# Capacity experts: routing and slot scatter moved into the preceding attention, results scattered from the slots to the output

## The reference

```python
x = _layernorm(x + _L1_attn_ref(x, ...))      # 16 heads of 8, Gaussian position bias
x = _layernorm(x + _L1_ffn_ref(x, gate_w, w1, w2))

# _L1_ffn_ref: 4096 tokens, 8 experts, capacity 160 slots each
probs = softmax(tokens @ gate_w)
expert_idx = argmax(probs)                     # one expert per token
mask1 = one_hot(expert_idx, E)
pos = cumsum(mask1, axis=0) - 1                # place of the token in its expert's queue
sec_mask = mask1[:, :, None] * one_hot(pos, CAP)    # places from 160 on are dropped
expert_input = einsum('tec,td->ecd', sec_mask, tokens)
h = relu(expert_input @ w1);  expert_output = h @ w2
out = einsum('tec,ecd->td', probs[:, :, None] * sec_mask, expert_output)
```

## Time and profile before

| | |
|---|---|
| median of 3 runs | 1858.01 us (1857.74 to 1858.42) |
| the profiled execution's own time | 1856.96 us |
| its span | 1855.2 us |
| mean granted TensorE clock | 0.936 of full |
| PE busy | 1522.6 us (82%) |
| DVE busy | 1325.1 us (71%) |
| ACT busy | 1047.6 us (56%) |
| POOL busy | 812.4 us (44%) |

### The profile page before, as it was taken

One profiled execution on the slowest core, in us unless ns is written; L12 is line 12 of the kernel. 1 busy time (PEld: TensorE's weight loads), 2 busy tenths in 40 slices (PEclk: granted clock), 3 DMA queues, 4 the chain that ended last, 5 costly groups with the idle time before them and its releaser, 6 DMA issues. The chain is left out here.

```text
span 1855.2 us, 37479 instructions
## 1 busy us (share of the span) xinstructions
PE 1522.6 (82%) x11749; PEld 858.2 (46%) x11749; DVE 1325.1 (71%) x3018; ACT 1047.6 (56%) x2241; POOL 812.4 (44%) x1161
## 2 busy tenths in 40 slices
PE   5899989899998999999688887489989998996050
PEld 3566656565665656656446565123333333323050
DVE  4777777777777777777678888377777777784115
ACT  2777767677676767767324444166666666665010
POOL 3656565656565565656525555212111211100625
PEclk8999999999999999999779999599999999998575
DMA  5000000000000000000000000400101010100117
GB/s 166 8 0 1 0 1 0 0 0 0 0 0 0 0 0 0 0 0 0 1 1 1 0 0 2 131 31 30 38 18 35 27 37 20 35 11 16 29 32 74
DMA packets 38861, 34.53 MB, mean 19 GB/s; under 512 B 6124, under 2 KB 35042, under 8 KB 38690
## 3 DMA queue, kind: packets, MB, share of 16 engines
q1 hardware_dynamic: 34946, 28.07, 5.1%
q0 software_dynamic: 2048, 2.77, 1.8%
q10 hardware_dynamic: 1824, 3.15, 0.5%
HBM read 22.43 MB, written 12.85 MB: 19 GB/s over the span
## 5 line engine op out<-in xcount | busy, mean ns | idle before, releaser
L1475 DVE TENSOR_REDUCE a_nm<-a_s 128x1 f16<-128x512 f32 x512 | 324.2, 687 | 59.3 <-PE a_s L1286 58.4
L532 ACT ACTIVATE prob<-score_ps,nmax 128x512 f32<-128x512 f32 (+3 forms) x512 | 265.3, 529 | 165.0 <-DVE nmax L595 161.6
L1406 ACT ACTIVATE a_pt<-a_st 128x1024 f32<-128x1024 f32 x256 | 260.5, 1021 | 116.3 <-PE a_st L1304 112.7
L129 POOL TENSOR_TENSOR gate<-mhalf 128x1 f32<-128x1 f32 (+1 forms) x276 | 57.0, 206 | 426.8 <-ACT k L565 252.0
L1286 PE MATMUL a_s<-a_kop,a_qop 128*128 128x512 f16 x512 | 198.7, 389 | 54.2 <-DVE a_nm L1475 37.4
L595 DVE TENSOR_REDUCE nmax<-score_ps 128x1 f32<-128x512 f32 (+3 forms) x512 | 220.9, 481 | 12.9 <-PE score_ps L438 7.2
L451 PE MATMUL pt_ps<-ident,prob 128*128 128x128 f32 x1280 | 189.3, 279 | 21.4 <-DVE pt L618 17.5
L451 PEld LDWEIGHTS pt_ps<-ident,prob 128*128 128x128 f32 x1280 | 140.5, 140 | 76.0 <-DVE pt L618 50.6
L623 DVE SCALAR_TENSOR_TENSOR q<-proj_ps,q_bias,q_mult 128x512 f32<-128x512 f32 x130 | 97.5, 750 | 102.4 <-PE proj_ps L406 96.2
L611 DVE TENSOR_SCALAR prob<-prob,rsum 128x128 f32<-128x128 f32 (+3 forms) x256 | 162.6, 698 | 2.3
L890 ACT ACTIVATE hid<-fps,b_cols 128x512 f32<-128x512 f32 x130 | 86.4, 687 | 126.9 <-PE fps L850 126.9
(11 more groups left out here) (344 smaller groups left out, 3526.1 us busy)
## 6 DMA issues: line engine op xcount, KB each, us to landing
a_qop<-q_parts SPq DMA_DIRECT2D x32, 128.0 KB
a_kop<-k_parts SPq DMA_DIRECT2D x128, 24.0 KB
x_tok<-in_L_attn_input_dram SPq DMA_DIRECT2D x4, 512.0 KB, 12.4
e_w<-in_L_ffn_w_dram SPq DMA_DIRECT2D x1, 2048.0 KB, 8.5
q_parts<-a_q_h SPq DMA_DIRECT2D x16, 128.0 KB
k_parts<-a_k_h SPq DMA_DIRECT2D x16, 128.0 KB
out_dram<-c_res SPq DMA_DIRECT2D x8, 256.0 KB, 3.7
w_raw<-in_L_attn_qkv_dram ACTq DMA_DIRECT2D x1, 1536.0 KB, 7.3
```

What stands on the lines that cost most here:

```text
L532: ins = nc.scalar.activation(prob[h][:, P_OFF[c]:P_OFF[c] + w], score_ps[u][:, col:col + w], ACT.Exp, bias=nmax[h][:, c:c + 1], accum_out= ...
L1406: nc.scalar.activation(pt[kc % 2][r][:, :, :], st_ps[r][:, :, :], ACT.Exp, scale=1.0 / SC).then_inc(exp_done[r], 1)
L1475: nc.vector.tensor_reduce(nm[g % 2][:, c, hh:hh + 1], s_ps[c % 2][:, :], AX.X, ALU.max, negate=True).then_inc(max_done[c % 2], 1)
```

## The change

- The router, the slot numbers and the scatters move into the second attention. New steps `RX` (transpose the normalised batch) and `RL` (router) stand at slots 13 and 14 of each batch for the batch behind. Slot numbers come in three instalments: batches 0 to 5 during the last batch (`shift`, `choose`, `RC` at slots 1, 2, 3), batch 6 in the tail, batch 7 at the tail's new last slot (`RD`). GpSimd scatters two chunks per slot from slot 4 of the last batch on, then four in the tail and four at its end.
- A scattered row is 130 wide: the token, its softmax weight, and its number plus one. The numbers come from a new table by a DMA of single elements, at slot 1 of the first batch; there `slot_rows` is also zeroed.
- The attention's `norm` writes `xn` in place of `x_tok`. GpSimd copies it into the wide rows, and works out what a second LayerNorm of it would be (a factor per row), which SyncE stores to the output for every token, slot or no slot.
- The last phase loads the slots in four parts, computes the experts, adds and normalises in the slots (80 partitions, 2 tiles per expert), and scatters each expert's two tiles straight to the output. Stages (1), (2) and (5) of before are gone from it, with `expert_rows` and the gathers.

```diff
-        MIDDLE = {4: "nm0", 8: "nm1", 9: "CT", 10: "OUT", 12: "nm2"}
+        MIDDLE = {4: "nm0", 8: "nm1", 9: "CT", 10: "OUT", 12: "nm2", 13: "RX", 15: "RD"}
-        END = {0: "ctx1", 1: "XT", 2: "Q", 4: "ctx2", 5: "K", ... 13: "V", 15: "nm3"}
+        END = {0: "ctx1", 1: "XT", 2: "Q", 3: "RC", 4: "ctx2", 5: "K", ... 13: "V", 14: "RL", 15: "nm3"}
+        EXPS_AT = {("last", 1): 0, ("tail", 0): 1, ("tail", 15): 2}
+        CHOSEN_AT = {("last", 2): 0, ("tail", 1): 1, ("tail", 15): 2}
...
# SyncE, attention
+                sp.dma_start(m.e_wg[:, :], io["L1_ffn_gate_w"]).then_inc(r.wg_in, 16)   # now first
...
+                if kind == "first" and at == 1:
+                    sp.dma_start(r.tri[:, :], io["c_tri"]).then_inc(r.tri_in, 16)
+                    sp.dma_start(r.rows[:, :, D + 1], io["c_tok"], allow_slow_non_contiguous=True).then_inc(r.tok_in, 16)
+                    sp.wait_ge(r.zeros_set, 1)
+                    sp.dma_start(r.slot_rows.rearrange("(p r) d -> p (r d)", p=P), r.zeros[:, :]).then_inc(r.zeroed, 16)
...
+            def norm(cb):
+                sp.wait_ge(r.rows_done, cb + 2)
+                sp.dma_start(out_rows[:, ds(cb * QC, QC), :], res[:, :, :]).then_inc(r.res_free, 16)
# TensorE, attention
+            def rows_t(kind, b, cb):
+                pe.wait_ge(ln_dve, SETUP_STEPS + cb + 1)
+                shared(kind, b, "RX")
+                for c in range(QC):
+                    mm = nc.tensor.transpose(misc[:, c * P:(c + 1) * P], xn[:, c, :], m.ident[:, :])
+                mm.then_inc(misc_mm, 1)
+            def router(kind, b, cb):
+                shared(kind, b, "RL")
+                for c in range(QC):      # 12 matmuls of 8 columns
...
# VectorE, attention: shift, choose, place as before, on 24, 4 and 4 chunks; RX's low half; logits copied
+            def logits(kind, b, cb):
+                used(kind, b, "RL")
+                nc.vector.tensor_copy(m_flat(r.logit)[:, ds(cb * QC * E1, QC * E1)], misc[:, 0:QC * E1]).then_inc(misc_out, 1)
# GpSimd, attention
             def output(kind, b, cb):
                 layer_norm_gpsimd(nc, pool, m, 2 * B + cb, mv, ve, rstd)
+                # four more small steps: scale[3] = (var * rstd * rstd + eps) ** -0.5
+            def norm(cb):
+                pool.wait_ge(ln_dve, SETUP_STEPS + cb + 1)
+                pool_gate(nc, m, slice(0, P))
+                nc.gpsimd.tensor_copy(into, xn[:, :, :])
+                pool.wait_ge(r.scale_steps, 4 * cb + 4)
+                pool.wait_ge(r.res_free, 16 * cb + 1)
+                nc.gpsimd.tensor_tensor(res[:, :, :], xn[:, :, :], scale[3]..., ALU.mult).then_inc(r.rows_done, 1)
...
+                if kind == "last" and at >= 4:
+                    scatter(range(2 * (at - 4), 2 * (at - 3)))
+                if kind == "tail" and at == 6:
+                    scatter(range(NCH - 2 * QC, NCH - QC))
# last phase
+            sp.wait_ge(r.scattered, 16 * NCH)
+            rows = r.slot_rows.rearrange("(t p) d -> p t d", p=HALF)
+            for q in range(4):
+                sp.dma_start(xe[:, 4 * q:4 * q + 4, :], rows[:, 4 * q:4 * q + 4, :]).then_inc(xe_in[q], 16)
+            def finish(e):        # VectorE: 2 scale-and-adds, 2 statistics, 2 aggregates, 1 sum
...
+            for e in range(E1):   # GpSimd
+                if e + 1 < E1:
+                    inverse_deviation(e + 1)
+                pool.wait_ge(out_ready, e + 1)
+                for t in (2 * e, 2 * e + 1):
+                    nc.gpsimd.indirect_dma_start(out=out_flat, out_offset=...to_token[:, t:t + 1]..., in_=res[:, t, :], ...)
```

More of the change, by code:

```diff
@@ L1122, in shared_use @@
                 if part in PARTS_OF[kind]:
-                    batch = {"ahead": b + 1, "own": b, "behind": b - 1}[part]
+                    batch = {"ahead": b + 1, "behind": b - 1}.get(part, b)
                     if name[-1] in "0123":
@@ L1130, in batch @@
                 behind, own = kind != "first", kind != "tail"
-                for at in range(SLOTS if own else 12):
+                for at in range(SLOTS):
                     g, s = divmod(at, G)
@@ new lines, in _, with shift @@
+            wide = lambda a, n: a.unsqueeze(2).to_broadcast([P, n, E1])
+            def logits(kind, b, cb):
+                used(kind, b, "RL")
+                nc.vector.tensor_copy(m_flat(r.logit)[:, ds(cb * QC * E1, QC * E1)], misc[:, 0:QC * E1]).then_inc(misc_out, 1)
+            def shift(h):
+                dve.wait_ge(misc_out, [use("middle", B - 2, "RL"), use("last", B - 1, "RL"), use("tail", B, "RL")][h] + 1)
+                hs, n = slice(ROUTED[h][0], sum(ROUTED[h])), ROUTED[h][1]
+                routing.step(nc.vector.tensor_reduce(r.lmax[:, hs], r.logit[:, hs, :], AX.X, ALU.max))
+                nc.vector.tensor_tensor(r.logit[:, hs, :], r.logit[:, hs, :], wide(r.lmax[:, hs], n), ALU.subtract).then_inc(r.shifted, 1)
@@ L1500, in _, with slot @@
+            def slot(kind, b, at):
+                if (kind, at) in EXPS_AT:
+                    shift(EXPS_AT[kind, at])
+                if (kind, at) in CHOSEN_AT:
+                    choose(CHOSEN_AT[kind, at])
+            schedule(dve, {"slot": slot, "RX": low("RX", xr_h, xr_l, r.rx_hi), "RL": logits, "RC": place("RC"), "RD": place("RD"), "setup": setup, "XT": low("XT", xt_h, xt_l, xt_hi), "V": values, "GB": gate_bias, "PZ": centres,
                            "scores": maxima, "ctx": context, "CT": low("CT", ct_h, ct_l, ct_hi), "OUT": output, "norm": norm})
@@ L1564, in _, with last_rows, moe_capacity_phase @@
+            def last_rows(kind, b, _):
+                scatter(range(NCH - QC, NCH))
+            schedule(pool, {"norm": norm, "RD": last_rows, "setup": setup, "prepared": first_values, "slot": slot, "Q": split("Q", q32, q_h, q_l, q_split, 1),
                             "K": split("K", k32, k_h, k_l, k_split, 2), "PZ": polynomial, "OUT": output})
-def moe_capacity_phase(nc, io, out, m):
+def moe_capacity_phase(nc, out, m):
     with ExitStack() as ctx:
```

440 lines of the change are left out of this document (213 added, 227 removed).

## The result

The changed kernel takes 1773.82 us (median of 4 runs, 1770.22 to 1774.86) against 1858.22: a ratio of 0.9544 [0.953, 0.9559], 84.4 us less. 1775 was predicted. The profiled execution, the slowest of the four, took 1774.86 us; it has a span of 1773.1 us and a granted clock of 0.956. Its span is 82.1 us shorter than that of before.

A forecast was written before the change was run, and what follows sets the result against it. It took GpSimd's issue of scatters and gathers to bound the last phase, and engines loaded against each other the attention. Last phase -100.1, attention +17: -83 from 1858.0 gives 1775 us; range 8 in 10, 1762 to 1797, likeliest case 1765 to 1787.

The forecast's parts named there:

- (a): Last phase, from VectorE's last norm: routing of batch 7 takes 8.6 us, bounds 7.5 and 11.
- (b): Last phase, after the routing: four scatters in place of 32, three intervals of 1.29 plus 2.1 to land, 6.0 us.
- (c): Last phase, before the experts: loading the first quarter of the slots takes 2.4 us, between 2.1 and 5.56.
- (d) and (e): Last phase, experts' start to the end: same matmuls, GpSimd paces at 3.2 us per expert; 37.2 us, bounds 33.5 and 41.
- RX and RL: Second attention, slots 13 and 14: these steps cost 0.8 us in each of six middle batches and the last, 5.6 us.
- First instalment: Last attention batch, slots 1 to 3: slot numbers for 24 chunks lose 7.0 us, bounds 4.3 and 9.
- Element-wise load: Attention, ahead of nm0: loading 4096 token numbers element by element costs 2 us, bounds 0 and 10.
- SyncE: Attention, slot 12: waiting for GpSimd's product before nm2's load costs 0.5 us in all, upper bound 2 per batch.
- GpSimd is slowed by VectorE: Third rival: scatters beside busy VectorE take 2.5 us each, inverse deviation and tail some 20 us late, 1796 us; chance 0.07.
- Slower than before: Rival: SyncE's wait for GpSimd's product makes every next attention batch's operands late, 1862 us; chance 0.03.
- It pays less: Rival: cheap rate everywhere in the attention, element load hidden, TensorE paces the end, 1765 us; chance 0.15.
- The attention pays more: Rival: operands 2 us late in seven batches, RX and RL at V's rate, element load at 8, about 1796; chance 0.18.

The follow-up runs named there:

- the first two sets: The changed kernel run again, unchanged, as the base of two later sets of experiments on other chips: 1787.68 us in each.

## Why the prediction was right, and where its parts were not

1773.8 against 1775 is closer than its parts deserve: the attention paid 5 us less than predicted and the last phase saved 4.5 less. That the two cancel is luck.

**The mechanism** was right. 28 scatters went under the attention, and they do not show there in the first measurement: the last batch takes 64.05 us with them and 63.78 in the run without. GpSimd has the time. With all 32 scatters behind the attention the last phase is 29.1 us longer, against 28 x 1.28 = 35.8 that they take to issue; the difference is that early chunks need not wait for batch 7's slot numbers: the first of the 32 starts 2.6 us behind the norm (1717.88 against 1715.26), not 9.05.

**(a) Routing of batch 7**: 8.6 predicted, 9.05 measured (1714.37 to 1723.42). Right, though the text takes 4.5 for the slot numbers and its sum 4.7. RX took 2.6 us for the 2.14 of CT, at a clock of 0.50 in a stretch where TensorE does almost nothing.

**(b) Four scatters**: 6.0 predicted, 7.8 measured. The three intervals are right (3.9); behind the last I took the 2.1 us landing of the earlier trace rows. The row is right for a DMA that a wait for its semaphore follows. The last scatter does land after 2.1 us. But a phase boundary follows, and all engines left it 3.9 us after the scatter's start. Putting the scatters behind the boundary brought 2.27.

**(c) Load**: 2.4 predicted, 2.8 measured, inside its bounds. With (a) and (b) it makes 19.7 us from the last norm to the first expert, for 17.

**(d) and (e) Experts to the end**: 37.2 predicted, 39.0 measured. The last scatter starts 35.1 us after the experts' start, for 34.8: GpSimd paces, as taken, by 3.1 us per expert for 3.2. Two errors cancel in it: a scatter of 80 rows takes 0.92 + 0.30 = 1.22 us (1.29 taken), the power on two columns 0.73 (0.6 taken). What was off is what follows the last scatter: it lands after 2.1 us, as taken, but the span ends 3.9 us after its start, where 2.4 were taken. That is the interval of (b) again, at the end of the block. So the step that failed in the last phase is one: the wait behind a scatter was priced by its landing where the end of a block follows, 1.8 and 1.5 us of the 4.5.

**RX and RL**: 5.6 predicted for seven batches, 1.9 measured for the six middle ones (0.31 each for 0.8) and 0.7 in the last. Over-sized: 0.8 was taken between 0.45, the cheap rate, and 1.4 by V (by V's own row, 1.07 for 0.69, it is 1.3), and V's 1.07 us are mostly a wait for TensorE, not work on VectorE. RX cost nothing in slot 13 and 0.1 in slot 14.

**First instalment**: 7.0 predicted with bounds 4.3 and 9; 9.0 measured, at the upper bound. The operations are as sized (7.7 us of VectorE for the 8.0 taken). What was missing is the clock: some 1.4 us of slot 4 come from TensorE's idling during place, and vanish when it is kept busy. And 3.5 us of the price, these 1.4 among them, are not the work's but the block's.

**Element-wise load**: 2 predicted, bounds 0 and 10; 0.1 measured. Its issue took 0.64 us, it landed 4.7 us later, and the first batch took 54.52 for 54.39: nothing waited for the load, which was issued at 1203 and used at 1645. By the Trainium skill (DMA: Bandwidth & Descriptors, Rules for kernel authors) each element of a strided last dimension becomes a descriptor of its own. The trace agrees: from 1202.5 to 1209.8 us it has 4172 packets of 4 bytes.

**SyncE**: 0.5 predicted, no cost measured. The store and the loads behind it in a middle batch:

```profile
1297.42 0.42 SPq L1270 DMA_DIRECT2D out_dram<-a_res  x1
1297.96 0.66 SPq L1265 DMA_DIRECT2D a_qop<-a_nm_t  x1
```

**Setup**: 1.2 predicted; 0.2 remain of the 1.6 once what comes from earlier phases is taken off.

**The rivals.** "GpSimd is slowed by VectorE" is refuted: 971 ns. The Trainium skill (SBUF — State Buffer, SBUF: two separate sides) states that VectorE locks GpSimd out in a two-port mode, or with two SBUF inputs while GpSimd reads SBUF. The reductions here read one operand, in PSUM, and the trace agrees as far as that goes: no scatter took over 1.21 us beside them. "Slower than before" never came near: no batch is late on operands. The output scatters land in 2.2 us in the median; one, the sixth, took 3.6, and nothing waited for it. "It pays less" was right of the attention, where RX and RL cost less than the cheap rate and the element load nothing, and wrong of the end, where GpSimd paces. "The attention pays more" was wrong in its own places, but in the first two sets the kernel takes 1787.7 us, inside the range of 1762 to 1797 and just outside the likeliest case's own, from a cause that no rival named. The reverse of the third rival is what exists there: not GpSimd held up by VectorE, but VectorE and ScalarE held up by late semaphore updates while GpSimd's scatters are in flight. The prediction has no term for this, and that it does not show in the first measurement is luck.

## What to carry to other kernels

Software-issued scatters can be hidden under another phase, but a dense train of them can hold up the other engines, and one measurement need not show it: time such a kernel on several chips, and try a wait between the scatters (here for all but one to have landed). Price a step by the engine that ends its slot, and a serial block also by what the idle TensorE loses in clock behind it. Put scatters whose landing must be awaited behind a phase boundary, not ahead of it. And before two profiles are compared by a median, see that it is taken over the same instructions in both.

## What was not expected of the hardware

- The same program takes 1773.8 us in the first measurement and 1787.7 in the first two sets, on two chips, while the kernel before differs by 2.6 us at most over all five sets of runs. The scatters land alike in all, 2.1 to 2.2 us for the last four.
- On those two chips semaphore updates of TensorE come 4 to 5 us, once 10 us, after its matmul has ended, while scatters are issued every 1.28 us, and the waiting engine starts 22 to 24 ns after the update. With a wait between the scatters (1.56 us apart in the mean) both stalls go (12.5 us of the kernel's time). That the recording plays a part is not ruled out.
- After a last scatter the boundary between phases lets engines through 3.9 us after its start, 1.6 later than a wait for the landing (2.27). The end of the program stands 3.9 us behind the start of its last scatter too (4.3 in the two runs with 150 filler matmuls).
- TensorE's clock fell from 1.00 to 0.52 during 5 us without work; behind it TensorE was busy 2.97 of 3 us at 0.50, then 3.58 of 4 at 0.88, then at 1.00 again.
